# A two-layer decoder on one NeuronCore: the cross attention's scores and weighted sums as three rounded products, with single buffers and another order of a step

## The chip, the core and the metric

The kernel runs on one core of a Trainium2 chip. The metric is device time in microseconds of one execution. The kernel before has a median of 2368.88 us over 3 runs.

## What is computed

Two layers, each a gated cross attention and a gated feed-forward part, on x of 8 x 256 x 512. The change lies in the second layer's cross attention (queries are the normalised x, keys and values come from a context of the same size; 16 heads of 128):

```python
x = x + jnp.tanh(g_xattn[1]) * cross(_layernorm(x), ctx_2048, Wq, Wk, Wv, Wo)

def cross(inputs_q, inputs_kv, Wq, Wk, Wv, Wo):
    q = (inputs_q @ Wq).reshape(b, sq, H, HD) * (1.0 / np.sqrt(HD))
    k = (inputs_kv @ Wk).reshape(b, skv, H, HD)
    v = (inputs_kv @ Wv).reshape(b, skv, H, HD)
    attn = jax.nn.softmax(jnp.einsum('bqhd,bkhd->bhqk', q, k), axis=-1)
    return jnp.einsum('bhqk,bkhd->bqhd', attn, v).reshape(b, sq, H * HD) @ Wo
```

## The kernel before

The program is five stages in a row: image attention, quantised feed-forward, cross attention, latent attention, experts. Each engine's instructions are written out by hand, with semaphores between them.

cross_attention (L1539) runs 32 steps: 4 groups of 4 heads, in each the 8 batch items. A product of split operands writes an f32 value as a rounded high part plus a rounded low part (type fp32r) and adds three products: high by low, high by high, low by high (split_product, L45). Projections already work so; scores (L203) and weighted sums (L286) are plain f32 matmuls, of which the profile records two pieces each.

In step s TensorE does, in this order (L1799 to L1832): scores of query tile 0 of item s; queries of item s+1; scores of tile 1; the transposes of tile 0's weights (att.turn); keys of s+1; transposes of tile 1; the first half of the values of s+1; in the first six steps (s+2 < 8) the transposes of x for s+2 (turn_x); weights times values (weigh); the second half of the values; outputs of item s. The projections, x's transposes and the outputs all go through a ring of two PSUM banks (use, L1703): a product waits until the one two before it was copied out.

VectorE (L1975) finds the peaks, inverts the sums, copies queries, keys, values (front, L1940) and half of the transposed weights, and adds the outputs to x. ScalarE (L1897) does the exponentials, the other half of the transposed weights, and all high parts. GpSimd (L1689) normalises the weights and forms the low parts of x and context (inputs_low, context_low). Weights (weights_high, weights_low) are split once a group: those of queries and keys at its predecessor's last but one step, of the values at its last, of the outputs in the first step. In the last 7 steps VectorE takes statistics of the finished rows (row_stats, L1959). SyncE (L1650) loads the inputs; in the first group it also stores the transposed x (store_turned), which later groups reload. Queries, keys and values have two buffers, the f32 inputs xt_f and ctx_f have arrays of their own. A step's wait for its inputs stands in:

```python
if s > 0:
    sp.wait_ge(ctx_lo_done, s)
sp.dma_start(ctx_f[:, :, :], ctx_t[s % BATCH]).then_inc(ctx_in, 16)
```

## Time and profile before

| | us |
|---|---|
| the three runs | 2367.17, 2368.88, 2374.07 |
| span of the profiled execution, first to last instruction | 2364.0 |
| TensorE busy | 2215.3 (94%) |
| VectorE / ScalarE / GpSimd busy | 1316.0 / 1000.6 / 794.9 |
| scores of the cross attention, 512 records (L203) | 121.8 |
| weights times values, 512 records (L286) | 117.5 |
| their stage, from its first context load to TensorE's last product | 668.61 to 1704.63 |

The profile gives the span of its own execution, not that execution's time. The median of the runs is 4.9 us above that span. Busy times of TensorE overlap from one record to the next.

### The profile page before, as it was taken

The numbers are of one execution on the slowest core, as the hardware profiler recorded it, in microseconds if no ns is written. First come the engines' busy times: TensorE is split into PE (matmuls) and PEld (weight loads), VectorE is DVE, ScalarE is ACT, GpSimd is POOL, SyncE is SP. The second block draws the span as 40 slices with busy tenths as digits, with TensorE's granted clock in tenths as the row PEclk, the third lists the DMA queues.
The fourth block names the chain that finished last, engine by engine and source line by source line (L and its number), as shares of the span: only waits on it lengthen the run. The fifth ranks groups of instructions, "written<-read, shape, count | busy, mean of one in ns | idle before, by whom it ended". The sixth has DMA issues, their size and how long they took to land. (4 is left out here: it accounts for less than half of the span.)

```text
span 2364.0 us, 42185 instructions
## 1 busy us (share of the span) xinstructions
PE 2215.3 (94%) x17406; PEld 1809.9 (77%) x17406; DVE 1316.0 (56%) x2355; ACT 1000.6 (42%) x1770; POOL 794.9 (34%) x687
## 2 busy tenths in 40 slices
PE   6999998689979999999999999999889999799997
PEld 4666676344458889889899999889767777699996
...
DMA packets 45342, 177.49 MB, mean 75 GB/s; under 512 B 5984, under 2 KB 5984, under 8 KB 38880
## 3 DMA queue, kind: packets, MB, share of 16 engines
...
## 5 line engine op out<-in xcount | busy, mean ns | idle before, releaser
L247 POOL TENSOR_TENSOR c_prob<-c_prob,c_inv_mass 128x512 f32<-128x512 f32 x128 | 130.5, 1041 | 437.9 <-DVE c_inv_mass L239 437.9
L229 ACT ACTIVATE c_prob<-c_s_ps,c_neg_peak 128x256 f32<-128x256 f32 x256 | 118.0, 473 | 360.5 <-DVE c_neg_peak L218 360.4
L47 PE MATMUL c_ring<-bc_xt_lo,bc_wq_hi 128*128 128x256 f32 x512 | 151.8, 296 | 5.4 <-POOL bc_xt_lo L1675 5.4
L47 PE MATMUL c_ring<-c_ctx_lo,c_w_hi 128*128 128x256 f32 x512 | 146.2, 286 | 0.0
L48 PE MATMUL c_ring<-bc_xt_hi,bc_wq_hi 128*128 128x256 f32 x512 | 145.9, 285 | 0.0
L49 PE MATMUL c_ring<-bc_xt_hi,bc_wq_lo 128*128 128x256 f32 x512 | 145.8, 285 | 0.0
L49 PE MATMUL c_ring<-c_ctx_hi,c_w_lo 128*128 128x256 f32 x512 | 143.0, 279 | 0.0
L48 PE MATMUL c_ring<-c_ctx_hi,c_w_hi 128*128 128x256 f32 x512 | 143.0, 279 | 0.0
L1679 POOL TENSOR_TENSOR c_ctx_lo<-c_ctx_f,c_ctx_hi 128x1024 fp32r<-128x1024 f32 x32 | 78.4, 2449 | 166.9 <-ACT c_ctx_hi L1868 166.9
L203 PE MATMUL c_s_ps<-c_kt,c_qt 128*128 128x256 f32 x512 | 121.8, 381 | 3.0 <-ACT c_prob L229 3.0
L1201 POOL TENSOR_TENSOR b_hw<-b_h,b_lnw 128x512 f32<-128x512 f32 x64 | 96.3, 1522 | 78.8 <-DVE b_h L1375 78.8
L1675 POOL TENSOR_TENSOR bc_xt_lo<-c_xt_f,bc_xt_hi 128x1024 fp32r<-128x1024 f32 x32 | 79.1, 2471 | 127.4 <-ACT bc_xt_hi L1862 127.4
L286 PE MATMUL c_o_ps<-c_prob_t,c_v 128*128 128x256 f32 x512 | 117.5, 383 | 0.9 <-ACT c_prob_t L276 0.9
L2052 DVE SCALAR_TENSOR_TENSOR x_res<-c_ring,c_gain,x_res 128x512 f32<-128x512 f32 x64 | 47.7, 750 | 114.0 <-PE c_ring L49 114.0
L295 DVE TENSOR_TENSOR c_o_lo<-c_o_ps,c_o_hi 128x1024 fp32r<-128x1024 f32 x32 | 39.2, 1224 | 127.5 <-ACT c_o_hi L291 127.5
L47 PE MATMUL c_ring<-c_w_lo,c_ctx_hi 128*128 128x512 f32 x256 | 110.0, 430 | 0.0
L286 PEld LDWEIGHTS c_o_ps<-c_prob_t,c_v 128*128 128x128 f32 x512 | 97.9, 192 | 15.5 <-issue 1.3
L1944 DVE COPY c_kt<-c_ring 128x512 f32<-128x512 f32 x64 | 44.2, 691 | 116.7 <-PE c_ring L49 116.7
L1944 DVE COPY c_qt<-c_ring 128x512 f32<-128x512 f32 x64 | 44.3, 692 | 116.1 <-PE c_ring L49 116.1
L203 PEld LDWEIGHTS c_s_ps<-c_kt,c_qt 128*128 128x128 f32 x512 | 94.8, 190 | 16.7 <-ACT c_prob L229 3.8
L3022 POOL DMA_INDIRECT out<-el_r,e_target x44 | 80.4, 1828 | 76.5 <-DMA out<-el_r,e_target 61.7
L47 PEld LDWEIGHTS c_ring<-bc_xt_lo,bc_wq_hi 128*128 128x128 f32 x512 | 99.2, 194 | 6.6 <-POOL bc_xt_lo L1675 5.8
...
## 6 DMA issues: line engine op xcount, KB each, us to landing
x_res<-b_w SPq DMA_DIRECT2D x48, 512.0 KB, 4.9
...
bc_raw<-c_w SPq DMA_DIRECT2D x16, 1024.0 KB, 5.9
c_ctx_f<-ctx_t SPq DMA_DIRECT2D x32, 512.0 KB, 3.5
c_xt_f<-xnt_scratch SPq DMA_DIRECT2D x24, 512.0 KB, 3.2
...
```

What stands on the lines that cost most here:

```text
L47: pe.matmul(out, lhs[0], rhs[1], start=first, stop=False)
L48: pe.matmul(out, lhs[0], rhs[0], start=False, stop=False)
L49: return pe.matmul(out, lhs[1], rhs[0], start=False, stop=last)
L203: mm = pe.matmul(self.s_ps[:, j, 0:w], q_of(u, j), k_of(u, j)[:, 0:w], start=mask is None, stop=True, skip_group_check=mask is not None)
L229: ins = act.activation(self.prob[:, u % 2, j, 0:w], self.s_ps[:, j, 0:w], ACT.Exp, bias=self.neg_peak[:, u % 2, j:j + 1], scale=self.scale ...
L247: pool.tensor_tensor(part, part, self.inv_mass[:, u % 2, js].unsqueeze(2).to_broadcast([P, 2, w]), ALU.mult).then_inc(self.prob_done, 1)
L286: mm = pe.matmul(out_of(g, j), v_of(g, j, t), self.prob_t[:, buf, t, j, :], start=(t == 0), stop=(t == TB - 1))
L1201: pool.tensor_tensor(hw[:, n % 2, cols], h[:, n % 2, cols], lnw[:, cols], ALU.mult).then_inc(hw_done, 1)
L1675: pool.tensor_tensor(xt_lo[:, :, :], xt_f[:, :, :], f32(xt_hi[:, :, :]), ALU.subtract).then_inc(xt_lo_done, 1)
L1679: pool.tensor_tensor(ctx_lo[:, :, :], ctx_f[:, :, :], f32(ctx_hi[:, :, :]), ALU.subtract).then_inc(ctx_lo_done, 1)
L1944: dve.tensor_copy(to, bank_of(f"f{k}", s)).then_inc(free_of(f"f{k}", s), 1)
L3022: pool.indirect_dma_start(out=out[:, :], out_offset=bass.IndirectOffsetOnAxis(ap=target[:, TB * j + t:TB * j + t + 1], axis=0), in_=r[:, j ...
```

## The change

Queries, keys, values and the transposed weights are each kept as a high and a low part (qt_hi, qt_lo and so on), in one buffer instead of two, and scores and weighted sums become split products. For that, ScalarE copies the high part out of PSUM (front_high, turned_high) and VectorE subtracts (front_low, turned_low). The f32 arrays xt_f and ctx_f now lie on xt_lo and ctx_lo, whose values are formed in place. So a load waits for the last product that reads the low part, and the low part waits for the store. TensorE's order becomes: scores 0, outputs of s-1, scores 1, transposes 0, queries, transposes 1, keys, x's transposes, weigh, values. The unused causal branches of Attention go too; line numbers after the class fall by 18 at first.

```diff
         self.prob = sb("prob", [P, 2, 4, SEQ])
-        self.prob_t = sb("prob_t", [P, turned_buffers, TB, 4, SEQ])
+        self.prob_hi, self.prob_lo = (sb(n, [P, TB, 4, SEQ], F32R) for n in ("prob_hi", "prob_lo"))
...
-            mm = pe.matmul(self.s_ps[:, j, 0:w], q_of(u, j), k_of(u, j)[:, 0:w], start=mask is None, stop=True,
-                           skip_group_check=mask is not None)
+            mm = split_product(pe, self.s_ps[:, j, :], q_of(u, j), k_of(j), True, True)
...
+    def turned_high(self, act, b, u, t):
+
+        act.wait_ge(self.t_ready, TB * (b * self.units + u) + t + 1)
+        to, of = self.turned(self.prob_hi, u, t)
+        act.activation(to, of, ACT.Copy).then_inc(self.turned_hi, 1)
+
+    def turned_low(self, dve, b, u, t):
+
+        dve.wait_ge(self.turned_hi, TB * (b * self.units + u) + t + 1)
+        to, of = self.turned(self.prob_lo, u, t)
+        dve.tensor_tensor(to, of, f32(self.turned(self.prob_hi, u, t)[0]), ALU.subtract).then_inc(self.turned_lo, 1)
+
...
+                mm = split_product(pe, out_of(j), v_of(j, t), (self.prob_hi[:, t, j, :], self.prob_lo[:, t, j, :]), t == 0, t == TB - 1)
...
+        self.xt_f = nc.alloc_sbuf_tensor_at("bc_xt_f", [P, C, SEQ], F32, offset=nc.sbuf_top)
...
-        xt_f, ctx_f = sb("xt_f", [P, C, SEQ]), sb("ctx_f", [P, C, SEQ])
         xt_hi, xt_lo = handed.xt_hi, handed.xt_lo
-        ctx_hi, ctx_lo = sb("ctx_hi", [P, C, SEQ], F32R), sb("ctx_lo", [P, C, SEQ], F32R)
-        qt, kt = sb("qt", [P, 2, 4, SEQ]), sb("kt", [P, 2, 4, SEQ])
-        v = sb("v", [P, 2, TB, 4 * HD])
+        ctx_lo, ctx_hi = sb("ctx_lo", [P, C, SEQ], F32R), sb("ctx_hi", [P, C, SEQ], F32R)
+        xt_f = handed.xt_f
+        ctx_f = nc.alloc_sbuf_tensor_at("c_ctx_f", [P, C, SEQ], F32, offset=nc.sbuf_base - 2 * 4 * C * SEQ)
+        qt_hi, qt_lo = sb("qt_hi", [P, 4, SEQ], F32R), sb("qt_lo", [P, 4, SEQ], F32R)
+        kt_hi, kt_lo = sb("kt_hi", [P, 4, SEQ], F32R), sb("kt_lo", [P, 4, SEQ], F32R)
+        v_hi, v_lo = sb("v_hi", [P, TB, 4 * HD], F32R), sb("v_lo", [P, TB, 4 * HD], F32R)
         o_hi, o_lo = sb("o_hi", [P, 4, SEQ], F32R), sb("o_lo", [P, 4, SEQ], F32R)
...
+        PLACES = (("o0", -1), ("o1", -1), ("f0", 1), ("f1", 1), ("d0", 0), ("d1", 0), ("f2", 1), ("f3", 1), ("xt0", 2), ("xt1", 2),
+                  ("dl", 0), ("f4", 1), ("f5", 1))
...
                 if s >= BATCH:
-                    sp.wait_ge(xt_lo_done, s)
+                    await_ready(sp, "f1", s - 1)
                     if s == BATCH:
                         sp.wait_ge(stored, 16 * BATCH)
                     sp.dma_start(xt_f[:, :, :], xnt_dram[s % BATCH]).then_inc(xt_in, 16)
                 if s > 0:
-                    sp.wait_ge(ctx_lo_done, s)
+                    await_ready(sp, "f5", s - 1)
                 sp.dma_start(ctx_f[:, :, :], ctx_t[s % BATCH]).then_inc(ctx_in, 16)
...
                 pool.wait_ge(xt_hi_done, s + 1)
+                if turned(s):
+                    pool.wait_ge(stored, 16 * (s + 1))
...
+                if here(s) and here(s + 1):
+                    context_low(s + 1)
+                if here(s):
                     att.normalise(pool, s, 1)
                 if here(s + 2):
                     inputs_low(s + 2)
-                    context_low(s + 2)
                 if s in (LATENT, LATENT + 1):
...
+            def outputs(s):
+                await_weights(s, WO)
+                pe.wait_ge(att.o_lo_done, s + 1)
+                for t in range(TB):
+                    use(f"o{t}", s, tokens((w_hi[WO], w_lo[WO]), o_hi, o_lo, t))
...
                 now, nxt = here(s), here(s + 1)
                 if now:
                     scores(s, 0)
+                if here(s - 1):
+                    outputs(s - 1)
+                if now:
+                    scores(s, 1)
+                    att.turn(pe, s, 0)
+                if nxt:
+                    queries(s + 1, 0)
+                    queries(s + 1, 1)
                 if s == LAST:
                     turn_rows(0)
                     turn_rows(1)
-                if nxt:
-                    queries(s + 1, 0)
-                    queries(s + 1, 1)
-                if now:
-                    scores(s, 1)
-                    att.turn(pe, s, 0)
+                if now:
+                    att.turn(pe, s, 1)
                 if nxt:
                     keys(s + 1, 0)
                     keys(s + 1, 1)
-                if now:
-                    att.turn(pe, s, 1)
-                if nxt:
-                    values(s + 1, 0)
                 if turned(s + 2):
                     turn_x(s + 2, 0)
                     turn_x(s + 2, 1)
-                if now:
-                    weigh(s)
-                if nxt:
-                    values(s + 1, 1)
                 if s == LAST:
                     latents()
                 if now:
-                    await_weights(s, WO)
-                    pe.wait_ge(att.o_lo_done, s + 1)
-                    for t in range(TB):
-                        use(f"o{t}", s, tokens((w_hi[WO], w_lo[WO]), o_hi, o_lo, t))
+                    weigh(s)
+                if nxt:
+                    values(s + 1, 0)
...
-                        act.wait_ge(xt_lo_done, s)
-                        act.wait_ge(stored, 16 * s)
+                        await_ready(act, "f1", s - 1)
...
+            def front_high(s, k):
+                await_ready(act, f"f{k}", s)
+                act.activation(front(k)[0], bank_of(f"f{k}", s), ACT.Copy).then_inc(front_hi_done, 1)
...
                     att.exponentials(act, s, 0)
-                if s == LAST:
-                    turned_high()
-                if here(s + 1) and (s + 1) % BATCH == 0:
+                if nxt and (s + 1) % BATCH == 0:
                     weights_high((s + 1) // BATCH, WV)
-                if now and s % BATCH == 0:
-                    weights_high(s // BATCH, WO)
                 if s == -1:
                     act.wait_ge(gate_in, 16)
                     act.activation(gain[:, :], gate_sb[:, :], ACT.Tanh).then_inc(gain_done, 1)
+                if now and nxt:
+                    context_high(s + 1)
                 if now:
                     att.exponentials(act, s, 1)
+                    att.turned_high(act, s, 0, 0)
+                    att.turned_high(act, s, 0, 1)
+                if now and s % BATCH == 0:
+                    weights_high(s // BATCH, WO)
+                if nxt:
+                    front_high(s + 1, 0)
+                    front_high(s + 1, 1)
+                if s == LAST:
+                    turned_high()
+                    rope_high()
                 if group_after(s) is not None:
                     weights_high(group_after(s), WQ)
                 if now:
-                    att.copy_turned(act, s, 0, 1, s % 2)
-                    att.copy_turned(act, s, 1, 1, s % 2)
-                if s == LAST:
-                    rope_high()
+                    att.turned_high(act, s, 1, 0)
+                    att.turned_high(act, s, 1, 1)
+                if nxt:
+                    front_high(s + 1, 2)
+                    front_high(s + 1, 3)
                 if turned(s + 2):
                     copy_inputs(s + 2)
                 if here(s + 2):
                     inputs_high(s + 2)
-                if now:
-                    if s > 0:
-                        await_ready(act, "o1", s - 1)
-                    att.output_high(act, s, 0, o_hi[:, :, :], att.o_ps[:, :, :].rearrange("p k (j q) -> p (k j) q", j=2))
-                if here(s + 2):
...
+            def front_low(s, k):
+                dve.wait_ge(front_hi_done, 6 * s + k + 1)
+                high, low = front(k)
+                dve.tensor_tensor(low, bank_of(f"f{k}", s), f32(high), ALU.subtract).then_inc(free_of(f"f{k}", s), 1)
...
                     att.find_peak(dve, s, 0)
-                if nxt:
-                    front(s + 1, 0)
+                    att.invert_mass(dve, s, 0)
+                if here(s - 1):
+                    add_to_x(s - 1)
+                if now:
+                    att.find_peak(dve, s, 1)
+                    att.turned_low(dve, s, 0, 0)
+                    att.turned_low(dve, s, 0, 1)
                 if s == -1:
                     late_stats(0)
                 if s >= LATENT:
                     row_stats(s - LATENT)
                 if now:
-                    att.invert_mass(dve, s, 0)
-                if nxt:
-                    front(s + 1, 1)
+                    att.invert_mass(dve, s, 1)
+                if nxt and (s + 1) % BATCH == 0:
+                    weights_low((s + 1) // BATCH, WV)
+                if nxt:
+                    front_low(s + 1, 0)
+                    front_low(s + 1, 1)
                 if s == -1:
                     late_stats(1)
-                if nxt and (s + 1) % BATCH == 0:
-                    weights_low((s + 1) // BATCH, WV)
                 if now and s % BATCH == 0:
                     weights_low(s // BATCH, WO)
-                if now:
-                    att.find_peak(dve, s, 1)
-                    att.copy_turned(dve, s, 0, 0, s % 2)
-                if nxt:
-                    front(s + 1, 2)
+                if s == LAST:
+                    turned_low()
+                if group_after(s) is not None:
+                    weights_low(group_after(s), WQ)
+                if now:
+                    att.turned_low(dve, s, 1, 0)
+                    att.turned_low(dve, s, 1, 1)
+                if nxt:
+                    front_low(s + 1, 2)
                 if s == -1:
                     late_stats(2)
-                if now:
-                    att.invert_mass(dve, s, 1)
-                if s == LAST:
-                    turned_low()
-                if nxt:
-                    front(s + 1, 3)
+                if nxt:
+                    front_low(s + 1, 3)
                 if s == -1:
                     late_stats(3)
```

TensorE, one step in the middle of the stage, before. c_s_ps are scores, c_t_ps transposed weights, c_ring projections and outputs, c_o_ps weighted sums; "..." leaves out the rest of a product:

```order
L203 MATMUL c_s_ps<-c_kt,c_qt 128x256 x4
L47 MATMUL c_ring<-bc_xt_lo,bc_wq_hi 128x256
...
L203 MATMUL c_s_ps<-c_kt,c_qt 128x256 x4
L259 MATMUL c_t_ps<-ident,c_prob 128x128 x8
L47 MATMUL c_ring<-c_ctx_lo,c_w_hi 128x256
...
L286 MATMUL c_o_ps<-c_prob_t,c_v 128x256 x8
L47 MATMUL c_ring<-c_w_lo,c_ctx_hi 128x512
...
L47 MATMUL c_ring<-c_w_lo,c_o_hi 128x512
```

and in the change:

```order
L47 MATMUL c_s_ps<-c_kt_lo,c_qt_hi 128x256
...
L47 MATMUL c_ring<-c_w_lo,c_o_hi 128x512
...
L47 MATMUL c_s_ps<-c_kt_lo,c_qt_hi 128x256
...
L242 MATMUL c_t_ps<-ident,c_prob 128x128 x8
L47 MATMUL c_ring<-bc_xt_lo,bc_wq_hi 128x256
...
L47 MATMUL c_o_ps<-c_prob_lo,c_v_hi 128x256
...
L47 MATMUL c_ring<-c_w_lo,c_ctx_hi 128x512
```

The outputs moved between the two scores, the queries behind the first transposes; 8 plain matmuls of a step became 24 rounded ones, twice.

VectorE in step 7 of the change, where a new group's weights for the values are split (c_w_lo):

```order
L205 TENSOR_SCALAR c_neg_peak<-c_peak 128x2
L259 TENSOR_TENSOR c_prob_lo<-c_t_ps,c_prob_hi 128x4x128 x2
L223 RECIPROCAL c_inv_mass<-c_mass 128x2 x2
L1965 TENSOR_TENSOR c_w_lo<-bc_raw,c_w_hi 128x2048
L1961 TENSOR_TENSOR c_qt_lo<-c_ring,c_qt_hi 128x512 x2
L259 TENSOR_TENSOR c_prob_lo<-c_t_ps,c_prob_hi 128x4x128 x2
```

The inversion of tile 1's sums now stands behind two subtractions that wait for ScalarE, and the weights' subtraction directly behind it.

GpSimd at the stage's start and in step 0 of the change, with its waits (the names are those of an earlier stage's semaphores, which are used again; a_mean_steps is xt_hi_done, a_biases_in is stored):

```order
L1680 TENSOR_TENSOR bc_xt_lo<-bc_xt_f,bc_xt_hi 128x1024 [waits a_biases_in,a_mean_steps]
L1684 TENSOR_TENSOR c_ctx_lo<-c_ctx_f,c_ctx_hi 128x1024 [waits a_rows_in]
L1680 TENSOR_TENSOR bc_xt_lo<-bc_xt_f,bc_xt_hi 128x1024 [waits a_biases_in,a_mean_steps]
L231 TENSOR_TENSOR c_prob<-c_prob,c_inv_mass 128x512 [waits a_x_in0] x2
L1684 TENSOR_TENSOR c_ctx_lo<-c_ctx_f,c_ctx_hi 128x1024 [waits a_rows_in]
```

The first wait is new, and the context's subtraction moved between the two normalisations.

## Rows read from the trace of the kernel before

**Rows 1.** Windows of the cross attention: us; per engine busy us and (records); TensorE clock; DMA share; GB/s.

```profile
1100.00:1200.00 100.00, 100.00 (x614) 90.08 (x613) 44.29 (x75) 30.95 (x68) 31.27 (x21) 1.00 0.15 53
```

**Rows 2.** Timeline of TensorE, one step of the loop: start us, us, engine, line, operation, count.

```profile
1267.32 0.39 PE L47 MATMUL c_ring<-c_w_lo,c_o_hi 128*128 128x512 f32 x1
...
1272.92 1.89 PE L203 MATMUL c_s_ps<-c_kt,c_qt 128*128 128x256 f32 x8
...
1274.46 0.47 PE L47 MATMUL c_ring<-bc_xt_lo,bc_wq_hi 128*128 128x256 f32 x1
...
1280.39 1.89 PE L203 MATMUL c_s_ps<-c_kt,c_qt 128*128 128x256 f32 x8
...
1282.91 0.36 PE L47 MATMUL c_ring<-c_ctx_lo,c_w_hi 128*128 128x256 f32 x1
...
1288.65 1.04 PE L259 MATMUL c_t_ps<-ident,c_prob 128*128 128x128 f32 x8
...
1289.45 0.48 PE L47 MATMUL c_ring<-c_w_lo,c_ctx_hi 128*128 128x512 f32 x1
...
1292.33 3.62 PE L286 MATMUL c_o_ps<-c_prob_t,c_v 128*128 128x256 f32 x16
...
1295.59 0.59 PE L47 MATMUL c_ring<-c_w_lo,c_ctx_hi 128*128 128x512 f32 x1
...
1298.59 0.39 PE L47 MATMUL c_ring<-c_w_lo,c_o_hi 128*128 128x512 f32 x1
```

**Rows 3.** Timeline of VectorE: a peak in that step, two subtractions from PSUM in the last.

```profile
1273.98 0.69 DVE L215 TENSOR_REDUCE c_peak<-c_s_ps 128x2 f32<-128x512 f32 x1
1687.03 1.27 DVE L1969 TENSOR_TENSOR bc_xt_lo<-c_ring,bc_xt_hi 128x512 fp32r<-128x512 f32 x2
```

**Rows 4.** Timeline of ScalarE in that step: first exponential, copy of the transposed weights.

```profile
1274.97 0.47 ACT L229 ACTIVATE c_prob<-c_s_ps,c_neg_peak 128x256 f32<-128x256 f32 x1 [6.33 <-DVE c_neg_peak L218]
1284.26 0.61 ACT L276 ACTIVATE c_prob_t<-c_t_ps 128x512 f32<-128x512 f32 x1
```

**Rows 5.** Timeline of GpSimd in that step: the normalisation.

```profile
1278.56 2.04 POOL L247 TENSOR_TENSOR c_prob<-c_prob,c_inv_mass 128x512 f32<-128x512 f32 x2 [7.43 <-DVE c_inv_mass L239]
```

**Rows 6.** The stage's start: GpSimd and SyncE timelines; DMA issues (KB each, us to landing).

```profile
672.76 2.35 POOL L1675 TENSOR_TENSOR bc_xt_lo<-c_xt_f,bc_xt_hi 128x1024 fp32r<-128x1024 f32 x1 [8.79 <-ACT bc_xt_hi L1862]
...
673.33 0.37 SPq L1634 DMA_DIRECT2D xnt_scratch<-c_xt_f  x1
...
xnt_scratch<-c_xt_f SPq DMA_DIRECT2D x1, 512.0 KB, 11.1
...
xnt_scratch<-c_xt_f SPq DMA_DIRECT2D x6, 512.0 KB, 2.6
```

**Rows 7.** Step 0: TensorE timeline, and a window at the clock after it.

```profile
706.87 2.69 PE L203 MATMUL c_s_ps<-c_kt,c_qt 128*128 128x256 f32 x8 [2.67 <-ACT c_prob L229]
...
708.50:711.50 3.00, 3.00 (x14) 2.71 (x13) 1.95 (x2) 1.03 (x1) 0.63 (x1) 0.50 0.00 0
```

**Rows 8.** DMA issues of step 2's start: two weight loads behind a context load.

```profile
bc_raw<-c_w SPq DMA_DIRECT2D x2, 1024.0 KB, 6.9
c_ctx_f<-ctx_t SPq DMA_DIRECT2D x1, 512.0 KB, 3.8
```

**Rows 9.** Groups by line and shape, 690 to 1700 us: the weights' subtraction on VectorE.

```profile
L1948 DVE TENSOR_TENSOR c_w_lo<-bc_raw,c_w_hi 128x2048 fp32r<-128x2048 f32 x10 | 24.4, 2437 | 7.8 <-ACT c_w_hi L1842 7.8
```

**Rows 10.** Timelines of GpSimd and VectorE in the last step.

```profile
1691.99 2.37 POOL L1699 TENSOR_TENSOR bc_wq_lo<-c_next_raw,bc_wq_hi 128x1024 fp32r<-128x1024 f32 x1 [2.83 <-ACT bc_wq_hi L1891]
1692.20 2.21 DVE L82 TENSOR_TENSOR bc_row_tmp<-bc_row_rstd 128x24 f32<-128x24 f32 x1
```

**Rows 11.** Last steps: row statistics on VectorE; TensorE's first and last record of step 31.

```profile
1682.12 1.28 DVE L1499 BATCH_NORM_STATS2 bc_stats<-x_res 128x6 f32<-128x512 f32 x2
...
1679.39 1.89 PE L203 MATMUL c_s_ps<-c_kt,c_qt 128*128 128x256 f32 x8
...
1704.63 0.40 PE L49 MATMUL c_ring<-c_w_hi,c_o_lo 128*128 128x512 f32 x1
```

186 lines of the change are left out of this document (82 added, 104 removed).

## The prediction

> **What bounds the kernel now.** I read four views, in this order. The busy time by 100 us windows comes first: inside the cross attention TensorE is busy for all of a window at full clock, with the vector engines under half [rows 1]. So in this stage TensorE's own queue is the clock, and a microsecond saved there is saved whole unless it turns into a wait. The timeline of TensorE comes second: one step of the loop, from the output product of one batch item to that of the next, is 1267.32 to 1298.59, 31.27 us [rows 2]. The reader should see the starts only: a record's length overlaps its successor, so a price is the distance to the next start. Third, the timelines of VectorE, ScalarE and GpSimd give the prices of the helpers and how far behind TensorE they answer [rows 3 to 5]. Last come the ends of the stage, where TensorE does wait [rows 6, 7, 11]. Nothing outside cross_attention changes.
>
> **TensorE's own work, a saving.** Eight plain scores and eight plain weighted products a step become 48 rounded matmuls of 256 columns. In the step shown, the first scores take 1272.92 to 1274.46 (1.54), the second 1280.39 to 1282.91 less the 0.79 of its transposes (1.73), the weighted sum 1292.33 to 1295.59 (3.26). The first rounded matmul after a plain one also comes late: 0.18 in the queries and 0.20 in the values. Together 6.91 us. The keys show the rounded price: 48 matmuls in 5.74 us, 0.119 each [rows 2], in the same 128x256 form and with another stationary operand each time, as in the new products. 48 x 0.119 = 5.69. Queries 5.75, keys 5.74, transposes 2 x 0.80, values and outputs 5.60 each, new products 5.69: the step is 29.99 us, 1.28 less. Steps 1 to 30 keep this form: **-38.4 us**. A plain record (two per product) costs 0.2135, 0.107 for each 256 columns of one pass. The Trainium skill ("FP8 and Floating Point Precision", TensorE Precision Notes) says true FP32 is four passes through the array, so three products would be worth three quarters of the plain price. The rows say five sixths; by that rule the saving would be larger, and it is a rival below.
>
> **Where the conversions lie.** Every copy from PSUM becomes a copy on ScalarE (0.60 [rows 4]) and a subtraction on VectorE, 0.64 each by the nearest row, a subtraction from PSUM of the same size [rows 3]. I walked the queues with these prices, from T, the start of a step's scores. New order: scores to 1.4, outputs of the step before to 7.0, second scores to 8.4, transposes to 9.2, queries to 15.0, transposes to 15.8, keys to 21.5, weights times values, values. The tight chain is that of the second transposes. The peak starts 1.06 after the second scores start, the exponentials 0.99 later and take 1.9 [rows 3, 4], so they end at 11.0. Only now does ScalarE round the first transposes (to 12.0), VectorE subtracts (to 12.8) and inverts the sums, and GpSimd normalises in 2.04 [rows 5]: halves at 14.1 and 15.1. TensorE wants them at 15.15 and 15.55. It holds with 1.05 and 0.45 us to spare: cost nothing in a plain step. A ring bank is free 1.5 us after its product, against 2.8 us until it is needed: nothing, except in the steps that also transpose x, where that product is only 0.6 long: 1.0 of waiting for 0.44, **+2.8** over five steps.
>
> **The start: +9.7.** The rounded input is now formed in place over the array that a DMA stores, so GpSimd's first subtraction waits for that store. Before, it began at 672.76, before the store was even issued (673.33), and the store landed 11.1 us later, behind two weight loads [rows 6]. Bounds: a store with nothing ahead takes 2.6, so 676.0, and 11.1 gives 684.4. The context load that shared the end of that traffic now comes later, so I take 682.5, near the upper row.
>
> **The same store in later steps.** It is issued at T+0.65, behind the context load, which itself now waits for the values. Nearest rows: 2.6 alone [rows 6], 3.8 for a load with more behind it [rows 8]. I take T+4.85; then 2.35 of subtraction and 2.04 of normalising end at 9.3, where the first transposes want them at 8.85: 0.45 in steps 1 and 3 to 6, **+2.2**. In step 2 two weight loads (6.9 [rows 8]) are issued between. Bounds are 0 and, by the 11.1, 9; I take a landing at T+10, a wait of 5.7 and 2.0 of halved clock behind it: **+7.7**.
>
> **Halved clock.** After 2.7 us of idle before 706.87 the granted clock is 0.50 from 708.5 to 711.5 [rows 7], 1.2 instead of 2.4 GHz: half of the work of these 3 us and a little at both ends is lost, 1.7 us.
>
> **Step 0: -0.3.** There are no outputs to do between the two scores, so TensorE waits for the peak and the first exponentials, from T+1.4 to about T+9 (before, queries lay there and 2.7 were left [rows 7]). I get 37.1 against 37.44 before.
>
> **Weights of the values, steps 7, 15, 23: +9.9.** Their subtraction (2.4 us [rows 9]) now stands between the inversion of the sums and the q halves, at the moment when GpSimd normalises. A VectorE subtraction of two SBUF tensors that starts while GpSimd works is held until GpSimd ends: 1692.20, 2.21 us for a tiny operation, beside 1691.99, 2.37 us [rows 10]. Whichever comes first, the other loses: either the second transposes wait for 2.3 more, or the bank of the queries comes free late for the keys. 3.3 us for each. "SBUF — State Buffer" of the Trainium skill (shared port pair) calls this an exclusive lock held for the whole instruction. The trace agrees. Without such a lock the three would cost about 1.3 each, and the sum 6 us less.
>
> **Row statistics, steps 25 to 30: +5.1.** 1.28 us [rows 11] now stand between the subtraction and the inversion, in the tight chain, whose spare 0.45 it uses up: 0.85 a step.
>
> **The last step: +7.8.** It was 1679.39 to 1704.86 [rows 11]; now it holds the outputs of step 30 (5.6) besides, and ends with weighted sum, ScalarE, VectorE, outputs with nothing between. By the walk, with the second transposes at 15.6 and about 3.5 of halved clock, 33.3.
>
> **Sum.** -38.4 + 2.8 + 9.7 + 2.2 + 7.7 - 0.3 + 9.9 + 5.1 + 7.8 = **+6.5 us**. The profiled span of 2364.0 becomes 2370.5; the median of the runs lies 4.9 above that span, so 2375.4 us. A measurement of this kernel can tell 0.3%, 7.1 us, from no change: 2361.8 to 2376.0. The forecast lies inside, near the upper edge.
>
> **The rivals.**
> A, slower: the spare 0.45 us is not there. Place: the second normalisation. If the chain from the second scores to GpSimd is 1 us longer than walked (ScalarE and VectorE hand over twice, and each handover was a gap I took as about 0.05), each of the 30 steps loses 0.55, +16: 2392. It decides from 0.45 us upward. For it: the rows of before show only one handover. Against: each duration is from a row.
> B, faster: the stores and the weight subtraction hide. With landings as for a lone store the start costs 3.2, step 2 and the others nothing: 16.4 less, 2359. Against it: the 11.1 us.
> C, faster, the page's rule taken as mechanism: the rounded matmul costs only its pass, 0.107 instead of 0.119, 48 x 0.012 = 0.57 a step, 30 steps, 17 less: 2358. Against it: every rounded matmul in [rows 2] is at 0.117 or more.
> D: the change does not do what it says, and the new products run at the plain record's 0.2135: 48 x 0.095 x 30 = +137, 2512. Same form at 0.119 already excludes it nearly.
>
> **Numbers.** Forecast case 0.62 (its own errors, some 6 us, put 0.34 of it inside 0.3%, 0.28 above), A 0.20, B 0.13, C 0.04, D 0.01. Of B and C 0.03 stay within the bound, and A's mild form adds 0.01 there: faster 0.14, same 0.38, slower 0.48. The range reaches from 2360, near B, to 2388, most of A: 2 in 10 are left out.
>
> **What would show it.** Right: sixteen undisturbed steps at 30.0 us start to start; the first rounded queries near 685; one TensorE wait for GpSimd of 5 us or more in step 2; short waits for GpSimd's normalisation in steps 7, 15, 23 and from 25; a wait of 7 us in step 0. Wrong: steps at 30.5 or more with a wait before the second transposes each time (A); queries starting before 678 (B); new products at 0.107 (C). I would be wrong in kind if the time moved outside the cross attention.

## The result, and the profile after

The changed kernel takes 2392.49 us (median of four runs, 2385.32 to 2395.12), the kernel before 2368.03 in the same comparison: a ratio of 1.0097, 95% interval 1.0078 to 1.0116. It is slower by 24.5 us, where 6.5 were forecast. In the two profiled executions the span goes from 2364.0 to 2389.9 us, 25.9 more.

First TensorE's queue in a plain step (18) of the changed kernel, to be laid beside [rows 2]. Columns: start us, us, engine, line, operation.

```profile
1286.35 0.28 PE L47 MATMUL c_s_ps<-c_kt_lo,c_qt_hi 128*128 128x256 f32 x1
...
1287.78 0.40 PE L47 MATMUL c_ring<-c_w_lo,c_o_hi 128*128 128x512 f32 x1
...
1293.38 0.28 PE L47 MATMUL c_s_ps<-c_kt_lo,c_qt_hi 128*128 128x256 f32 x1
...
1294.82 1.03 PE L242 MATMUL c_t_ps<-ident,c_prob 128*128 128x128 f32 x8
...
1295.61 0.36 PE L47 MATMUL c_ring<-bc_xt_lo,bc_wq_hi 128*128 128x256 f32 x1
...
1301.43 1.03 PE L242 MATMUL c_t_ps<-ident,c_prob 128*128 128x128 f32 x8
1302.22 0.36 PE L47 MATMUL c_ring<-c_ctx_lo,c_w_hi 128*128 128x256 f32 x1
...
1307.96 0.29 PE L47 MATMUL c_o_ps<-c_prob_lo,c_v_hi 128*128 128x256 f32 x1
...
1310.84 0.39 PE L47 MATMUL c_ring<-c_w_lo,c_ctx_hi 128*128 128x512 f32 x1
...
1316.44 0.28 PE L47 MATMUL c_s_ps<-c_kt_lo,c_qt_hi 128*128 128x256 f32 x1
```

Read the starts: 1.43 + 5.60 + 1.44 + 0.79 + 5.82 + 0.79 + 5.74 + 2.88 + 5.60 = 30.09 us, no wait in it, against 31.27. The part of the change that was meant to shorten TensorE's work did so. The loss is in what TensorE waits for; the waits of that stage (us in total, times, longest):

```profile
PE c_t_ps L242 <- POOL c_prob L231: 27.8, 27, 5.6
PE c_ring L47 <- POOL bc_xt_lo L1680: 14.8, 1, 14.8
PE c_s_ps L47 <- ACT c_prob L213: 8.8, 1, 8.8
PE c_ring L1764 <- DVE c_kt_lo L1961: 7.5, 7, 1.1
```

27 waits for GpSimd's normalised probabilities, none of them in the 15 plain steps (most come in pairs, one for each half of a transpose), and the one at the start for GpSimd's first subtraction. Step by step (start of one step's first scores to the next's, from TensorE's timeline; "forecast" is the prediction's terms on the old length; for step 31 the prediction counts to 0.23 us behind the last matmul's start, so its 33.3 stands here as 33.1):

| steps | before | forecast | after | after, profiled again (e10) |
|---|---|---|---|---|
| start of step 0 | 696.5 | 706.2 | 705.3 | 703.3 |
| 0 | 37.44 | 37.1 | 37.85 | 38.04 |
| 1, 3, 4, 5 | 32.75 | 32.5 | 33.60, 33.61, 33.61, 33.41 | 33.92, 33.49, 33.79, 33.69 |
| 2 | 32.75 | 39.7 | 39.33 | 41.26 |
| 6 | 31.27 | 30.4 | 31.31 | 31.59 |
| 7, 15, 23 | 31.27 | 33.3 | 33.64, 33.79, 35.09 | 34.50, 33.90, 35.11 |
| 8 to 14, 16 to 22, 24 | 31.27 | 29.99 | 30.10 | 30.10 |
| 25, 28, 29, 30 | 31.27 | 30.84 | 30.74, 31.02, 30.73, 30.74 | 30.74, 31.01, 30.74, 30.74 |
| 26, 27 | 31.27 | 30.84 | 31.93, 34.11 | 31.94, 34.10 |
| 31, to the start of the last matmul | 25.2 | 33.1 | 34.0 | 34.0 |

From the stage's first transpose to the first scores of the next attention it is 1051.8 us before and 1072.2 after: +20.4. Of the other 5.5 of the span's 25.9, 5.2 arise in the experts at the end, and the runs below show that they are scatter.

**The store.** At the start SyncE issues it behind two weight loads, as before; now GpSimd waits for it. In step 1 it is issued at T+0.62 behind a context load; in step 2 two weight loads stand between. SyncE and GpSimd of the changed kernel at the start, in step 1 (T = 743.15) and in step 2 (T = 776.75):

```profile
673.26 0.37 SPq L1637 DMA_DIRECT2D xnt_scratch<-bc_xt_f  x1
...
682.03 2.34 POOL L1680 TENSOR_TENSOR bc_xt_lo<-bc_xt_f,bc_xt_hi 128x1024 fp32r<-128x1024 f32 x1 [19.26 <-DMA xnt_scratch<-bc_xt_f]
...
743.77 0.38 SPq L1637 DMA_DIRECT2D xnt_scratch<-bc_xt_f  x1
...
748.90 2.41 POOL L1680 TENSOR_TENSOR bc_xt_lo<-bc_xt_f,bc_xt_hi 128x1024 fp32r<-128x1024 f32 x1 [22.56 <-DMA xnt_scratch<-bc_xt_f]
751.27 2.04 POOL L231 TENSOR_TENSOR c_prob<-c_prob,c_inv_mass 128x512 f32<-128x512 f32 x2
...
778.32 0.42 SPq L1637 DMA_DIRECT2D xnt_scratch<-bc_xt_f  x1
...
787.57 2.34 POOL L1680 TENSOR_TENSOR bc_xt_lo<-bc_xt_f,bc_xt_hi 128x1024 fp32r<-128x1024 f32 x1 [29.19 <-DMA xnt_scratch<-bc_xt_f]
```

GpSimd's subtraction starts 0.1 to 0.2 us behind the landing: at 682.0 (682.5 taken), at T+5.75 in step 1 (T+4.85 taken), at T+10.8 in step 2 (T+10 taken). It stands ahead of the normalisation in GpSimd's queue, so in these steps a later landing is a longer wait of TensorE before the first transposes.

**A hold that the prediction did not see.** VectorE and GpSimd in step 27, and in step 7:

```profile
1566.75 2.94 POOL L1689 TENSOR_TENSOR bc_latent<-c_next_raw,bc_latent 128x1280 fp32r<-128x1280 f32 x1 [6.30 <-ACT bc_latent L1882]
...
1573.11 2.38 POOL L1684 TENSOR_TENSOR c_ctx_lo<-c_ctx_f,c_ctx_hi 128x1024 fp32r<-128x1024 f32 x1
```

```profile
1566.86 2.85 DVE L205 TENSOR_SCALAR c_neg_peak<-c_peak 128x2 f32<-128x2 f32 x1
...
1573.88 1.63 DVE L205 TENSOR_SCALAR c_neg_peak<-c_peak 128x2 f32<-128x2 f32 x1
```

```profile
957.46 2.41 POOL L1684 TENSOR_TENSOR c_ctx_lo<-c_ctx_f,c_ctx_hi 128x1024 fp32r<-128x1024 f32 x1 [1.48 <-ACT c_ctx_hi L1873]
962.90 4.07 POOL L231 TENSOR_TENSOR c_prob<-c_prob,c_inv_mass 128x512 f32<-128x512 f32 x2 [3.04 <-DVE c_inv_mass L223]
```

```profile
957.51 2.38 DVE L205 TENSOR_SCALAR c_neg_peak<-c_peak 128x2 f32<-128x2 f32 x1
...
962.80 2.27 DVE L1965 TENSOR_TENSOR c_w_lo<-bc_raw,c_w_hi 128x2048 fp32r<-128x2048 f32 x1
```

The peak scaling is two numbers a partition and takes 0.17 us nearly everywhere (median of 128: 169 ns; 18 of the 128 take 0.31 us or more). Here its record ends with GpSimd's: 1566.86 + 2.85 = 1569.71 beside 1566.75 + 2.94 = 1569.69, and 957.51 + 2.38 = 959.89 beside 959.87. It is held for as long as GpSimd's subtraction runs, and the exponentials wait for it. Step 0 has two such holds, 1.68 and 2.21 us. In step 7 the opposite happens too: VectorE's weight subtraction starts 0.10 us ahead of GpSimd's normalisation, which then takes 4.07 us for its two halves, not 2.04 (3.07 for the first, 1.04 for the second). In the kernel before, the same subtraction of 2.94 us ended at 1555.42, before that step's first scaling at 1556.11.

Step 15 has the same instructions as step 7, but ScalarE rounds the weights 0.36 us later, so GpSimd's subtraction begins 0.31 us behind the scaling, and nothing is held (T = 1192.36):

```profile
1201.84 0.17 DVE L205 TENSOR_SCALAR c_neg_peak<-c_peak 128x2 f32<-128x2 f32 x1
```

```profile
1202.15 2.40 POOL L1684 TENSOR_TENSOR c_ctx_lo<-c_ctx_f,c_ctx_hi 128x1024 fp32r<-128x1024 f32 x1 [1.84 <-ACT c_ctx_hi L1873]
1205.85 4.07 POOL L231 TENSOR_TENSOR c_prob<-c_prob,c_inv_mass 128x512 f32<-128x512 f32 x2 [1.30 <-DVE c_inv_mass L223]
```

Its second transposes start 1.4 us earlier than step 7's (T+16.62 against T+18.00), and yet it is the longer step, 33.79 against 33.63. The rest is the clock, in the windows behind the wait of step 15, first of the changed kernel, then of the run e2 below, whose step 15 has the same instructions and takes 32.35 us (columns: the window, its length, the busy time of PE, PEld, DVE, ACT and POOL with their records, granted clock, DMA share, GB/s):

```profile
1210.36:1212.36 2.00, 2.00 (x12) 2.00 (x11) 1.17 (x2) 1.09 (x2) 0.00 (x0) 0.52 0.05 8
1212.36:1214.36 2.00, 2.00 (x13) 2.00 (x12) 0.12 (x1) 0.00 (x0) 0.00 (x0) 0.63 0.00 0
```

```profile
1208.97:1210.97 2.00, 2.00 (x20) 2.00 (x19) 1.07 (x2) 1.09 (x2) 0.00 (x0) 1.00 0.06 20
```

So, against 30.10, the weights' conversion alone costs 2.25 us in such a step, a held scaling 1.28 more (step 7, whose clock stayed at 1.00), and a fallen clock another 1.4 to 1.5 (steps 15 and 23).

### The profile page after: what moved, and what is told of

Same layout as the page of the kernel before. It is cut to its first block and busy times, and to the rows that moved or that the text cites. A ratio compares the mean times of both kernels' runs of the same rounds, so it can differ in the third digit from the quotient of the medians.

```text
span 2389.9 us, 43410 instructions
## 1 busy us (share of the span) xinstructions
PE 2188.9 (92%) x17918; PEld 1808.7 (76%) x17918; DVE 1360.1 (57%) x2419; ACT 1138.6 (48%) x2026; POOL 793.2 (33%) x687
## 5 line engine op out<-in xcount | busy, mean ns | idle before, releaser
L1680 POOL TENSOR_TENSOR bc_xt_lo<-bc_xt_f,bc_xt_hi 128x1024 fp32r<-128x1024 f32 x32 | 76.6, 2393 | 398.9 <-ACT bc_xt_hi L1869 206.9
L259 DVE TENSOR_TENSOR c_prob_lo<-c_t_ps,c_prob_hi 128x512 fp32r<-128x512 f32 x128 | 82.4, 686 | 78.2 <-ACT c_prob_hi L253 77.0
L1961 DVE TENSOR_TENSOR c_kt_lo<-c_ring,c_kt_hi 128x512 fp32r<-128x512 f32 x64 | 44.2, 691 | 106.4 <-ACT c_kt_hi L1877 106.4
L47 PE MATMUL c_ring<-c_w_lo,c_o_hi 128*128 128x512 f32 x256 | 102.0, 399 | 2.4 <-DVE c_o_lo L277 2.4
L48 PE MATMUL c_ring<-c_w_hi,c_o_hi 128*128 128x512 f32 x256 | 101.7, 397 | 0.0
L49 PE MATMUL c_ring<-c_w_hi,c_o_lo 128*128 128x512 f32 x256 | 101.5, 397 | 0.0
L1961 DVE TENSOR_TENSOR c_v_lo<-c_ring,c_v_hi 128x512 fp32r<-128x512 f32 x64 | 44.3, 692 | 100.5 <-ACT c_v_hi L1877 100.5
L48 PE MATMUL c_ring<-c_w_hi,c_ctx_hi 128*128 128x512 f32 x256 | 101.3, 396 | 0.0
L49 PE MATMUL c_ring<-c_w_hi,c_ctx_lo 128*128 128x512 f32 x256 | 101.3, 396 | 0.0
L1877 ACT ACTIVATE c_kt_hi<-c_ring 128x512 fp32r<-128x512 f32 x64 | 38.2, 597 | 130.4 <-PE c_ring L49 130.4
```

Of the source, the lines that this page charges most:

```text
L47: pe.matmul(out, lhs[0], rhs[1], start=first, stop=False)
L48: pe.matmul(out, lhs[0], rhs[0], start=False, stop=False)
L49: return pe.matmul(out, lhs[1], rhs[0], start=False, stop=last)
L259: dve.tensor_tensor(to, of, f32(self.turned(self.prob_hi, u, t)[0]), ALU.subtract).then_inc(self.turned_lo, 1)
L1680: pool.tensor_tensor(xt_lo[:, :, :], xt_f[:, :, :], f32(xt_hi[:, :, :]), ALU.subtract).then_inc(xt_lo_done, 1)
L1877: act.activation(front(k)[0], bank_of(f"f{k}", s), ACT.Copy).then_inc(front_hi_done, 1)
```

## The experiments

A gain is given for the stretch named above (first transpose to the next attention's first scores; 1072.2 us in the changed kernel, 1075.7 in its second profile), or for steps, which repeat to 0.02 us where nothing of DMA is in them and the clock does not fall. Where it can fall they do not: with the same instructions step 7 took 33.63, 34.82, 35.18 and 34.50 us (changed kernel, e1, e2, e10), step 15 took 33.79, 33.86, 32.35 and 33.90. Runs e1 to e8 are one profiled execution each beside one or two of the kernel before (2371.34, then 2372.12 us); e9 to e11 are timed.

### e1: the stores ahead

```diff
             load_inputs(0)
+            store_turned(0)
             load_weights(0, WV)
...
-                if turned(s - 1):
-                    store_turned(s - 1)
+                if turned(s):
+                    store_turned(s)
                 load_inputs(s)
```

> The queue of SyncE is changed alone: the store of step s's transposed input is issued before the context load of step s (which waits for the previous step's values), not one step later behind it, and the first store stands ahead of the weight loads. Theory A (the landing of the store holds GpSimd's subtraction, and with it the probabilities): the first scores start about 8 us earlier than the 705.30 us of the changed kernel, step 2 falls from 39.33 to about 32.2 us, steps 1, 3, 4 and 5 fall from 33.60 to about 32.2 us each; 20 us in all. Theory B (the extra of steps 1, 3, 4, 5 comes from VectorE, which normalises an input tile for 1.0 us ahead of the peaks, and only step 2 and the start are the store's): steps 1, 3, 4, 5 stay at 33.3 to 33.6 us; 14 us in all.

Measured: the first scores at 694.5 instead of 705.3 (of the 10.8, 3.7 lie before the stage), steps 1 to 5 at 32.23 each, step 6 at 30.10, step 0 at 36.45 instead of 37.85 (its first scaling is no longer held), step 7 at 34.82 (its clock fell); the stretch 1051.7, 20.5 less. Theory A; VectorE's input normalisation costs nothing. SyncE and GpSimd of this run, start and step 0:

```profile
667.88 0.33 SPq L1637 DMA_DIRECT2D xnt_scratch<-bc_xt_f  x1
...
671.03 2.34 POOL L1681 TENSOR_TENSOR bc_xt_lo<-bc_xt_f,bc_xt_hi 128x1024 fp32r<-128x1024 f32 x1 [11.87 <-DMA xnt_scratch<-bc_xt_f]
...
689.80 0.33 SPq L1637 DMA_DIRECT2D xnt_scratch<-bc_xt_f  x1
...
692.55 2.41 POOL L1681 TENSOR_TENSOR bc_xt_lo<-bc_xt_f,bc_xt_hi 128x1024 fp32r<-128x1024 f32 x1 [16.84 <-DMA xnt_scratch<-bc_xt_f]
```

Issued with no other transfer close ahead, the store lands in 2.6 to 3.3 us, and GpSimd, which begins its subtraction then, does so in a gap of its work. So all that steps 1 to 6 took beyond 32.23 (30.10 in step 6) was the store's. The run took 2378.15 us, 14 less than the changed kernel, not 20: see e10.

### e2: row statistics behind the inversion

```diff
-                if s >= LATENT:
-                    row_stats(s - LATENT)
                 if now:
                     att.invert_mass(dve, s, 1)
+                if s >= LATENT:
+                    row_stats(s - LATENT)
```

> VectorE alone: in steps 25 to 30 the two row statistics (1.27 us) stand behind the inversion of tile 1's sums, not ahead of it. Theory A (they make the second transposes 1.41 us instead of 0.79): these go back to 0.79 in steps 25, 28, 29 and 30, 0.6 us a step; steps 26 (31.93) and 27 (34.11) keep what they have beyond that, since that comes from GpSimd's latent subtractions of 2.4 and 2.9 us at the steps' heads, which hold VectorE's peak scaling. 3 to 4 us in all. Theory B (steps 26 and 27 are long because the statistics and the held peak scaling add up): both fall below 31 us, 6 us in all.

Measured: steps 25, 28, 29, 30 at 30.10; 26 at 30.75; 27 at 31.50; the last step 30.0 instead of 34.0 (it has two row statistics as well, which neither theory nor the prediction had counted); the stretch 1062.0, 10.2 less. Neither theory is right. The delays add in one chain from which one spare is taken: a quiet step lost 1.28 of statistics less 0.64 of spare. In step 26 the second scaling is held 1.36 - 0.17 = 1.19 us more: 1.28 + 1.19 - 0.64 = 1.83, and 31.93 - 30.10 is 1.83. In step 27 it is held 1.63 - 0.17 = 1.46 more and also starts 0.49 later in the step (T+9.17 against T+8.68 in step 26, behind the first tile's held scaling): 1.28 + 1.46 + 0.49 - 0.64 = 2.59. (Without the statistics the same sums give 0.55 and 1.31; e2 leaves 0.65 and 1.41, so they hold to 0.1.) The step lost 4.01. The other 1.42 is the clock: in e3, below, the same wait (queries to second transposes 7.81 us, 7.80 here) is not followed by a lower clock, and step 27 takes 32.69 us, 2.59 more than a plain one. The changed kernel's windows behind that wait, then the one of e3 at the same place (columns as above):

```profile
1583.00:1585.00 2.00, 2.00 (x11) 2.00 (x11) 0.66 (x2) 1.08 (x2) 0.00 (x0) 0.50 0.03 8
1585.00:1587.00 2.00, 2.00 (x15) 2.00 (x15) 0.63 (x2) 0.00 (x0) 0.00 (x0) 0.78 0.00 0
```

```profile
1572.00:1574.00 2.00, 2.00 (x19) 2.00 (x18) 0.86 (x2) 0.15 (x2) 0.00 (x0) 1.00 0.00 0
```

So one wait can cost 2.6 or 4.0 us: the level of 1.2 instead of 2.4 GHz for some 3 us behind it is not there every time. What decides it no run here shows.

### e3: WV's conversion behind the queries' splits

```diff
                 if now:
                     att.exponentials(act, s, 0)
-                if nxt and (s + 1) % BATCH == 0:
-                    weights_high((s + 1) // BATCH, WV)
...
                     front_high(s + 1, 0)
                     front_high(s + 1, 1)
+                if now and nxt and (s + 1) % BATCH == 0:
+                    weights_high((s + 1) // BATCH, WV)
...
                     att.invert_mass(dve, s, 1)
-                if nxt and (s + 1) % BATCH == 0:
-                    weights_low((s + 1) // BATCH, WV)
...
                     front_low(s + 1, 0)
                     front_low(s + 1, 1)
+                if now and nxt and (s + 1) % BATCH == 0:
+                    weights_low((s + 1) // BATCH, WV)
```

(Group 0's weights stay where they were.)

> The rounding (ScalarE) and the subtraction (VectorE) of the next group's WV weights stand behind the queries' splits, not between the two tiles' exponentials and ahead of the queries' splits. Theory A (they hold tile 1's probabilities, in part because GpSimd's normalisation took 4.07 us for two halves beside VectorE's 2.3 us subtraction, against 2.04 elsewhere): steps 7, 15 and 23 fall from 33.64, 33.79 and 35.09 us to 30.1 to 31, 10 to 12 us in all. Theory B (the work only moves on to the second transposes' split and the keys' split): they stay above 32.5 us, under 4 us in all.

Measured: steps 7, 15, 23 at 31.03, 31.02, 31.01, 9.5 us less; the stretch 1061.9, 10.3 less. Theory A; GpSimd's normalisation is back at 2.04. What is left, 0.92 a step, is one scaling held 1.62 to 1.64 us by the context subtraction. That begins at T+7.91 in these steps and at T+5.71 in plain ones, because VectorE subtracts the keys' weights (2.28 us, the end of step 6's queue) ahead of the first peaks. Of the 9.5 us, 2.9 are the clock, which stayed at its upper level in steps 15 and 23 here; step 27 lost 1.42 less for the same reason.

### e4: a fourth product

```diff
-            mm = split_product(pe, self.s_ps[:, j, :], q_of(u, j), k_of(j), True, True)
+            split_product(pe, self.s_ps[:, j, :], q_of(u, j), k_of(j), True, False)
+            mm = pe.matmul(self.s_ps[:, j, :], q_of(u, j)[1], k_of(j)[1], start=False, stop=True)
```

(and the same in the weighted sums.)

> A fourth product, low by low, is added in the scores and in the weighted sums, 16 matmuls of 256 columns a step, in the changed kernel's order; nothing is left out. Theory A (a plain step is bound by TensorE throughout, each product costs what the three cost now, 1.43/12 = 0.119 us): 1.9 us a step, 61 us in all, about 2453 us, the plain step from 30.10 to 32.0. Theory B (the added products partly fill gaps that the other engines leave, as in steps 1 to 7 and 25 to 30): under 45 us. By this the three products save, against plain f32 of 6.53 us a step (1.54 + 1.72 + 3.27), only what 0.119 a product leaves: 5.75 us for three, 7.7 for four, so f32 is cheaper than four products.

Measured: the plain step 32.01, 1.91 more for 16 matmuls, 0.119 each; steps 0 to 30 together 52.6 more, 2440.18 us. For the plain steps theory A to the hundredth. The sum is between the two: in steps 25, 28, 29 and 30 only 1.67 are added, in step 27 nothing (33.65 against 34.11), since there the products lie partly in a wait. The price of one more rounded product is now known with nothing else changed: 3 cost 5.75 a step, 4 cost 7.66, plain f32 6.53 (6.91 with what follows it late). Three are 0.8 to 1.2 us a step cheaper than plain f32, four 0.8 to 1.1 dearer. The plain price is from the queue of the kernel before; no run puts plain f32 into the new order.

### e5: no peak scaling

```diff
-            dve.tensor_reduce(peak, self.s_ps[:, js, :], AX.X, ALU.max).then_inc(self.peak_found, 1)
-            dve.wait_ge(self.peak_found, 2 * n + (half + 1))
-            dve.tensor_scalar(neg_peak, peak, -self.scale, None, ALU.mult).then_inc(self.peak_done, 1)
+            dve.tensor_reduce(self.neg_peak[:, u % 2, js], self.s_ps[:, js, :], AX.X, ALU.min).then_inc(self.peak_done, 1)
...
-                act.activation(front(k)[0], bank_of(f"f{k}", s), ACT.Copy).then_inc(front_hi_done, 1)
+                act.activation(front(k)[0], bank_of(f"f{k}", s), ACT.Copy, scale=-SCALE if k < 2 else 1.0).then_inc(front_hi_done, 1)
```

(The low half of the queries is `bank * -SCALE - high` in one instruction, the exponential's scale is -1.)

> The changed kernel with VectorE's peak scaling (128x2, SBUF to SBUF) gone: the queries are split already multiplied by minus the scale, the peaks are taken as a minimum straight into the bias, and the exponential runs at scale -1. Theory A (the small scaling is what GpSimd's subtractions hold: 2.08, 2.85, 1.36 and 1.63 us in steps 26 and 27 in place of 0.17): step 26 falls from 31.93 to about 30.7 us and step 27 from 34.11 to 32.7 or less, the level of their statistics alone; plain steps stay at 30.10, since TensorE is their bound. Theory B (GpSimd holds VectorE whatever stands there, the reduction or the inversion too): steps 26 and 27 fall by under 0.5 us, and a reduction or an inversion takes over 1.5 us instead.

Measured: step 26 at 30.54, 27 at 30.53, the four quiet ones 30.53 to 30.81; and steps 7, 15 and 23 at 31.64 each, 2.0, 2.2 and 3.5 less, which was not expected. Step 0 is 36.22 instead of 37.85, its two holds gone. In step 7 the gain is the hold (1.28) and 0.71 of a shorter chain; step 15 had no hold, and its gain is that 0.71 and 1.44 of clock; step 23 gains by all three. The shorter chain is a confounder everywhere: with the scaling gone even the steps 25, 29 and 30, which had no hold, are 0.20 shorter. It is too small for steps 26 and 27 (1.4 and 3.6 less, of the latter 1.42 clock). The stretch is 1058.5, 13.7 less. Theory A. GpSimd and VectorE in step 27 of this run:

```profile
1559.34 2.94 POOL L1686 TENSOR_TENSOR bc_latent<-c_next_raw,bc_latent 128x1280 fp32r<-128x1280 f32 x1 [6.30 <-ACT bc_latent L1879]
1562.25 2.03 POOL L228 TENSOR_TENSOR c_prob<-c_prob,c_inv_mass 128x512 f32<-128x512 f32 x2
```

```profile
1558.74 1.28 DVE L202 TENSOR_REDUCE c_neg_peak<-c_s_ps 128x2 f32<-128x512 f32 x2
1560.57 0.17 DVE L220 RECIPROCAL c_inv_mass<-c_mass 128x2 f32<-128x2 f32 x1 [0.55 <-ACT c_prob L210]
1561.48 0.17 DVE L220 RECIPROCAL c_inv_mass<-c_mass 128x2 f32<-128x2 f32 x1 [0.75 <-ACT c_prob L210]
```

Beside the same 2.94 us of GpSimd a reduction from PSUM takes its 0.68 and a reciprocal 0.17. All 128 reductions of this run lie between 676 and 693 ns. What is held is the form of the instruction, not VectorE as such. The Trainium skill ("SBUF — State Buffer", Who interferes with whom) says so: `tensor_scalar` may take the port pair that VectorE shares with GpSimd, a reduction never does on this chip, and a `tensor_tensor` contends when both inputs are in SBUF; the one that starts later waits for the other's whole instruction. The trace agrees with all of it (2.85 against 0.17; 4.07 against 2.04).

### e6, e7, e8, e9: the moves together

e6 is e1 + e2 + e3; e7 adds the weighted sums ahead of the latents in step 31 (`weigh(LAST)`, then `latents()`, their splits on ScalarE and VectorE in the same order); e8 adds e5; e9 adds this, on TensorE:

```diff
                 if turned(s + 2):
                     turn_x(s + 2, 0)
-                    turn_x(s + 2, 1)
                 if now:
                     weigh(s)
+                if turned(s + 2):
+                    turn_x(s + 2, 1)
```

> The moves of the first three experiments together: stores early, statistics behind the inversion, WV's rounding and subtraction behind the queries' splits. Theory A (independent waits, their gains add): from the first input transpose of the cross attention to its hand-over 20.5, 10.3 and 12.7 us less, some 43 us less than the changed kernel, and 22 less than the kernel before: about 2346 us. Theory B (they cover one another, or a fourth wait shows): less than 35 us.

Measured: the stretch 1032.1, 40.1 less, where the three alone give 20.5 + 10.2 + 10.3 = 41.0; 2347.52 us. Theory A: three separate waits.

> As the run of the three moves, and in the last step the weighted sums stand ahead of the latents again (on TensorE, and their splits on ScalarE and VectorE), so that the latents' 2.9 us lie beside the output's split. Theory A (the last output product waits for the split, about 2 us, with nothing to do): the last step is 2 to 3 us shorter than in the run of the three moves. Theory B (the wait is that of the rows' transposes and their splits, so the order of the two does not matter): under 0.5 us.

Measured: the start of the last matmul 30.8 us into the last step instead of 32.1, the next attention's first scores 14.0 instead of 15.6 us behind it: 2.9 us. The size is theory A's, but only 1.3 of it lies in the last step, where theory A put all. The time did not show it (2347.34).

> As the run before it, and without the peak scaling. Theory A (the scaling held by GpSimd is what is left of the waits in steps 26 and 27): both come to 30.1 to 30.3 us, from 30.75 and about 31.5; the other steps are unchanged; 2 us in all. Theory B (another VectorE instruction is held in its place): they stay.

Measured: steps 6 to 30 all at 30.10, also 7, 15, 23, 26 and 27; the stretch 1024.7, 4.6 less; 2339.09 us. Theory A for steps 26 and 27. It had the other steps unchanged and 2 us in all; steps 7, 15 and 23 fell too, by 0.92 each, the held scaling that e3 had left there.

> As the run of all moves, and on TensorE the second input transpose of a step stands behind the weighted sums (steps 0 to 5), not directly behind the first. Theory A (the pair takes 2.05 us for 1.6 us or less of work only since the second waits for its buffer of two): the wait is hidden, steps 1 to 5 fall from 32.22 to 30.9 to 31.6 us, 3 to 6 us in all. Theory B (ScalarE then copies the second tile late, ahead of the output's split, and the next step's output product waits for it): no gain, or up to 2 us lost a step. Against the kernel before, all moves: 2334 to 2340 against 2369, a ratio of 0.985 to 0.988.

Measured: steps 1 to 5 at 30.96 instead of 32.22, theory A; steps 0 to 5 are 7.5 us shorter, of which 1.8 come back in step 31 and behind it (the stretch is 1019.1, 5.7 less). Five runs: 2334.92 us (2328.33 to 2348.28) against 2366.29 of eleven runs of the kernel before, ratio 0.9859 (0.9838 to 0.9880).

### e10 and e11: what is scatter

> The changed kernel itself, unchanged, timed again. Theory A (its 24 us over the kernel before hold 18 to 20 of the cross attention and the rest is scatter of the experts' transfers at the end, which took 26.0 us from the last expert product to the end in the kernel before, and 26.1 to 31.8 in the changed kernel and its variants): the cross attention's steps repeat within 1 us, and the time lies between 2372 and 2395 us. Theory B (the 5 us at the end belong to the change): the stretch from the last expert product to the end stays at 31 us in the changed kernel, and the time at 2390 to 2395.

> The run of all moves again, timed: 2335 to 2343 us, its steps 6 to 30 at 30.10 us each, a ratio of 0.985 to 0.989 against the kernel before. What TensorE does in a plain step is then 30.10 against 31.27 us, and nothing waits there; a rival that sees the gain in another place (the experts, the first attention) expects the stretch of the cross attention to differ by under 30 us from the kernel before's.

Measured: e10 2389.04 us (2383.05 to 2392.41, six runs), ratio 1.0092 (1.0072 to 1.0112); steps as in the table above, the stretch 1075.7 (step 2 alone 1.9 longer than in the first profile: GpSimd's subtraction began 0.4 later, at T+11.2, and the granted clock stood at 0.50 for 10 us, from within the wait on, instead of for 4). So theory A's "within 1 us" fails in step 2, while its time and its end of the program come true. e11 2339.39 us (four runs), ratio 0.9885 (0.9863 to 0.9908), stretch 1024.8, steps 6 to 30 at 30.10. By the letter its rival was met, since the stretch is 27.0 us shorter than the kernel before's and the line was drawn at 30; but the whole time is only 26.9 shorter, so the line was drawn wrong, and all of the gain is in the stretch. From the experts' first product to the end of the span it is 316.9 us before, 322.1 in the changed kernel, 318.1 in the same kernel profiled again, and 317.6 to 320.1 in e2 to e8 and e11, but 332.8 in e1 and 331.9 in e9. Behind the last expert product's last matmul lie 16.4 us before, 21.5 in the changed kernel and 17.7 in the same kernel profiled again. So those 5 us are not the change's. The long ends go with long waits of GpSimd for the scattered output rows; in this order: the kernel before, the changed one, e9, e8:

```profile
POOL out L3022 <- DMA out<-el_r,e_target: 61.7, 21, 6.9
```

```profile
POOL out L3042 <- DMA out<-el_r,e_target: 68.1, 21, 6.8
```

```profile
POOL out L3048 <- DMA out<-el_r,e_target: 78.3, 21, 9.8
```

```profile
POOL out L3047 <- DMA out<-el_r,e_target: 57.1, 20, 6.2
```

The same 20 or 21 waits, 57 to 78 us in one execution or another (55.1 in e10). Among the short ends the order does not follow them: 61.7 beside 316.9, 57.1 beside 319.1. e9's profiled execution is its slowest run (2348.28 us), and e1's 332.8 explains why it showed 14 us less and not 20. Why the transfers at the end differ so was not tried.

## Why the prediction was wrong, point by point

The direction had the largest chance, 0.48 for slower, but the forecast itself lay inside 0.3% of no change; the time did not hold, nor did the range (2388 at most). Eight of the nine terms of the sum have the sign that was measured. Four steps of the prediction failed. The landing of the store in steps 1 and 3 to 6 was mis-sized (T+4.85 taken, T+5.75 measured: 4.3 us). The hold of the peak scaling by GpSimd was put at nothing, without a reason (2.6 us in steps 7 and 23, 3.1 in steps 26 and 27, up to 1.6 in step 0), and so was the fallen clock behind the waits of steps 15, 23 and 27 (4.3 together). TensorE's own step was walked 0.11 us too short (3.3 us in 30 steps). Together these are more than the 14.0 us that were missed; the conversion of the value weights, put at 3.3 a step, costs 2.25 by itself and gives 3.2 of it back. Rival A's price, 2392, is the time that was measured, but by accident: the wait in every plain step that it stands for is not there.

| term | forecast | measured |
|---|---|---|
| TensorE's own work, 30 steps | -38.4 | -35.1 (1.17 a step) |
| the x-transposes' buffer | +2.8 | +3.2 (32.23 - 30.10 against 32.75 - 31.27, five steps) |
| the start | +9.7 | +8.8 |
| step 0 | -0.3 | +0.4 |
| store, steps 1, 3 to 6 | +2.2 | +6.5 |
| store, step 2 | +7.7 | +7.1 (e10: 9.0) |
| value weights, steps 7, 15, 23 | +9.9 | +12.2 |
| row statistics, steps 25 to 30 | +5.1 | +4.1 (0.64 each, 0.92 in step 28), and 4.6 more in steps 26 and 27 |
| last step | +7.8 | +8.7 |
| sum | +6.5 | +20.5 (the stretch: +20.4) |

(Measured: the differences of the step table, against 30.10 for a step without the term, 32.23 for steps 1 to 5.)

- **The saving.** Right in kind. The walk took 0.1185 for a product (48 x 0.119 is 5.71, not 5.69) where it is 0.1198 (5.75 / 48), and the queries 5.75 where they take 5.82 or 5.83. A tenth of a microsecond a step, but 30 times: 3.3 us.
- **The tight chain.** Right, and this is the nearest thing to a test of the whole walk: the spare was put at 0.45 us and is 0.64 (1.28 of statistics cost 0.64). Rival A, a wait in every step, is refuted: 15 plain steps at 30.10, TensorE without a gap.
- **The store in steps 1 and 3 to 6.** The step that failed: "I take T+4.85". GpSimd's subtraction began at T+5.75. With no spare there, 0.9 us of landing became 0.9 of wait: 1.36 instead of 0.45 in step 1, 1.2 to 1.4 in the others. The nearest row for it (3.8 us for a load with more behind it) was one of a transfer that is itself first; a store that is second in the queue took 5.0 us. Step 2 and the start, where the upper row of 11.1 was taken as near, came out within 1 us (step 2 of e10 is 1.3 off: 0.4 of landing, the rest clock).
- **Step 0.** Forecast 0.3 shorter, measured 0.4 longer. The two held scalings (1.68 and 2.21 us) explain more than that: without them, in e5, the step is 1.6 shorter.
- **The value weights.** The two-sided lock was seen, 3.3 us each, and the sizes 3.5, 3.7 and 5.0 look near, but they are made of other things. The weights' conversion costs 2.25 (step 15 of e2: no hold, clock at 1.00). In steps 7 and 23 the lock strikes at a second place, 1.28: ScalarE's rounding of the weights delays the context's, and GpSimd's subtraction of the context meets VectorE's scaling. Steps 15 and 23 lose 1.4 to 1.5 by the clock. That the sum came within 2.3 us of the forecast is in part luck.
- **Steps 26 and 27.** The largest blind spot by kind, 4.6 us: the held scaling, and 1.42 of clock behind one of the waits. The prediction had [rows 10], a small VectorE operation held for 2.21 us, and used it for the weights alone; it never asked which other VectorE instruction of that kind stands in the tight chain. It is the first one, the peak scaling.
- **The last step.** 8.7 against 7.8, but not for the reasons walked, so the nearness is luck: e2 takes 4.0 of it away, two row statistics between the subtraction and the inversion, which the term "steps 25 to 30" had left out; e7 takes 1.3.
- **Rivals B, C and D** are refuted by the start (GpSimd waits till 682.03), by 0.119 a product (e4), and by the same number.
- **The size of the range.** Apart from the start and step 2 the sum took a walk's bare value for each term, and anything overlooked in a walk could only add. Six of the nine terms came out dearer than forecast and two cheaper (the start by 0.9, step 2 by 0.6), while "its own errors, some 6 us" treated them as independent; the misses add to 14.0. The row statistics came out 1.0 cheaper by themselves, and 3.6 dearer with the holds of steps 26 and 27.

Was it the arithmetic or the order? The products are worth at most 6.53 - 5.75 = 0.78 us a step by their own windows, and with what came late behind a plain one, all of the 1.17. None of the loss lies in them; it lies in the conversions' place in the other queues and in the store. With the waits taken away one by one the same products run at 2334.92 us: 1.4% faster than the kernel before, instead of 1.0% slower. Not all of this 1.4% is the arithmetic's: the wait that e9 takes away was in the kernel before too (0.44 us in its step 0), and no run gives the kernel before such moves.
